# Perceiver layer on one core: first group's output projection and layer norm moved into the last sampled-attention group, set-up spreads moved to GpSimd

## What is computed

```
x = x + xattn(ctx, ctx, layernorm(x))   # K, V, Q projections; 5 sampled keys a query; softmax; @ Wo.T + bo
x = x + attn(layernorm(x))              # q, k, v = short_conv(h @ W); 2 chunks of 16 rows, carried W_in, W_out; @ Wo
x = x + ffn(layernorm(x))               # the expert of the largest gate score

def short_conv(x, w):
    xp = jnp.pad(x, ((0, 0), (KSIZE - 1, 0), (0, 0)))
    y = sum((w[:, j] * xp[:, j:j + l, :] for j in range(KSIZE)))
    return y + x
```

## Time and profile before

| what | value |
|---|---|
| median of three runs | 1219.58 us (1213.76 to 1223.68) |
| profiled execution | 1217.85 us, span 1216.1 us |
| TensorE busy, mean granted clock | 1061.4 us (87% of the span), 0.904 |
| VectorE, ScalarE, GpSimd busy | 813.3, 494.7, 320.2 us |
| SyncE's first transfer of the sampled attention, the fast weights, the experts | 115.55, 482.96, 1087.55 us from the span's start |

### The profile page before, as it was taken

The page is one execution under the profiler, slowest core; times in us unless marked ns, Lnnn a source line. Parts: engine busy times, 40 slices in busy tenths (PEclk is TensorE's granted clock), DMA queues, the critical chain, the costliest instruction groups (busy, mean ns, idle before and its releaser), DMA issues. The chain is left out here.

```text
span 1216.1 us, 18598 instructions
## 1 busy us (share of the span) xinstructions
PE 1061.4 (87%) x6220; PEld 787.6 (65%) x6220; DVE 813.3 (67%) x1592; ACT 494.7 (41%) x954; POOL 320.2 (26%) x265
## 2 busy tenths in 40 slices
PE   5993999999999963698999999999999987875997
PEld 4883566666666652477878776968696876763443
DVE  4565286778778883357888787979688876633332
ACT  1220255776676774134444443434252534310110
POOL 0344376677577662000000000000000000011553
PEclk9997898989889975788999999999899987765999
DMA  4281410222021000100010101010010031046541
GB/s 153 87 333 59 82 42 1 59 58 57 2 58 35 18 18 32 56 1 35 1 53 1 53 2 54 1 53 2 2 53 1 18 105 70 36 159 261 158 144 58
DMA packets 59924, 75.12 MB, mean 62 GB/s; under 512 B 37758, under 2 KB 42302, under 8 KB 57792
## 3 DMA queue, kind: packets, MB, share of 16 engines
q1 hardware_dynamic: 52384, 53.05, 13.7%
q0 software_dynamic: 5152, 12.59, 3.2%
q10 hardware_dynamic: 2304, 8.39, 1.7%
HBM read 56.71 MB, written 22.81 MB: 65 GB/s over the span
## 5 line engine op out<-in xcount | busy, mean ns | idle before, releaser
L1196 POOL COPY fw_x<-fw_x 128x1024 f32<-128x1024 f32 x8 | 8.3, 1040 | 536.0 <-DMA xh_scr<-fw_x 502.4
L556 POOL TENSOR_TENSOR aw_wtent<-aw_tent,aw_e 128x1760 f32<-128x1760 f32 x32 | 100.7, 3145 | 114.1 <-DVE aw_e L552 114.1
L745 PE MATMUL aw_psum_kv<-all_xWv,aw_c 128*128 128x512 f32 x256 | 124.6, 633 | 0.0
L528 POOL TENSOR_TENSOR aw_tent<-all_const,all_ix 128x1760 f32<-128x1760 f32 x32 | 100.6, 3145 | 5.1 <-POOL aw_wtent L556 4.6
L851 ACT ACTIVATE aw_cT<-aw_psum_av 32x256 f32<-32x256 f32 x128 | 80.5, 629 | 38.7 <-PE aw_psum_av L774 37.6
L733 PE MATMUL aw_psum_kv<-aw_c,all_xWk 128*128 128x352 f32 x256 | 81.6, 474 | 9.5 <-POOL aw_A L632 9.5
L2020 PE MATMUL ex_psum_y<-ex_We,ex_gT 128*128 x184 | 85.0, 607 | 0.0
L745 PEld LDWEIGHTS aw_psum_kv<-all_xWv,aw_c 128*128 128x128 f32 x256 | 49.4, 203 | 52.9 <-issue 51.1
L539 DVE TENSOR_TENSOR aw_prod<-aw_tent,aw_psum_s 128x1760 f32<-128x1760 f32 x32 | 63.5, 1984 | 23.8 <-ACT aw_tent L534 17.3
L1510 PE MATMUL fw_psum_front<-all_xWo,fw_cT 128*128 128x512 f32 x128 | 66.0, 666 | 11.7 <-DMA fw_cT<-c_scr 11.4
L733 PEld LDWEIGHTS aw_psum_kv<-aw_c,all_xWk 128*128 128x128 f32 x256 | 49.0, 196 | 35.2 <-POOL aw_A L632 9.6
(11 more groups left out here) (265 smaller groups left out, 2256.7 us busy)
## 6 DMA issues: line engine op xcount, KB each, us to landing
ex_We<-expert SPq DMA_DIRECT2D x1, 8192.0 KB, 22.4
aw_craw<-ctx SPq DMA_DIRECT2D x8, 704.0 KB, 4.8
xh_scr<-fw_x SPq DMA_DIRECT2D x10, 512.0 KB, 3.6
pj_x<-x_tok SPq DMA_DIRECT2D x8, 512.0 KB, 3.6
q_scr<-pj_QT ACTq DMA_DIRECT2D x8, 512.0 KB, 2.9
aw_Qb<-q_scr SPq DMA_DIRECT2D x32, 128.0 KB, 3.4
c_scr<-aw_cT ACTq DMA_DIRECT2D x8, 512.0 KB, 2.7
fw_cT<-c_scr SPq DMA_DIRECT2D x8, 512.0 KB, 4.8
```

Source lines behind the costliest of these rows:

```text
L528: return nc.gpsimd.tensor_tensor(self.tent[r][:], bc(rows, 1, self.nu * NK), bc(ix, 2, self.wr), ALU.subtract)
L556: return eng.tensor_tensor(self.wtent[:], self.tent[r][:], bc(self.e[:].rearrange("p u k -> p (u k)"), 2, self.wr), ALU.mult)
L745: mm = nc.tensor.matmul(ps_kv[:, j % 2, :], rows, Wv[:, c, :], start=(c == 0), stop=(c == KC - 1))
```

## The change

It adds a class `Lead` that owns two buffers for the whole kernel: `wide` (four tiles of 128x1024, which also serves as `Qblk[0]`, the even groups' queries of the sampled attention) and `even` (which also serves as `cw[0]`, the even groups' context). In the last group of the sampled attention, whose buffers are the odd ones, the `Lead` steps for group 0 of the fast weights are put between the group's own: loads behind the last scores of group 6, y0 and y1 into the two idle PSUM banks of `ps_kv`, addition, layer norm, transposes, copy into `hT`. The loads of group 1 are issued there too. The fast phase marks those fills as done and starts at the convolution fills. The clearing and the 16 copies go from VectorE to GpSimd; VectorE keeps the sum of convolution weights (`wsum`), which ScalarE now waits for in place of `setup`.

```
+class Lead:
+        self.cT = wide[:, 0:n].rearrange(cols, c=KC)
+        self.xs, self.x1, self.h = (wide[:, j * n:(j + 1) * n].rearrange(cols, c=TT) for j in (1, 2, 3))
+        self.hT = even[:, 0:n].rearrange(cols, c=KC)
+    def load(self, sp):
+        sp.dma_start(self.cT, self.a["c_scr"][0]).then_inc(self.c_in.sem, 16)
+        sp.dma_start(self.xs, self.a["x_lb"][0].rearrange("p t d -> p t d")).then_inc(self.x_in.sem, 16)
+        sp.wait_ge(self.x1_done.sem, self.x1_done.at(0, 1))
+        sp.dma_start(self.cT, self.a["c_scr"][1]).then_inc(self.c_in.sem, 16)
+        sp.dma_start(self.xs, self.a["x_lb"][1]).then_inc(self.x_in.sem, 16)
+        sp.wait_ge(self.c_in.sem, self.c_in.at(1, 16))
+        sp.wait_ge(self.x_in.sem, self.x_in.at(1, 16))
+    def sums(self, dve):
+            self.nc.vector.tensor_tensor(self.x1[:, j, :], ring.bank(f"y{j}"), self.xs[:, j, :], ALU.add)
+    def enter(self, dve):
+        ch.link(nc.vector.tensor_tensor(self.x1, self.x1, bc(self.k["weights"]["xbo"][:], 1, TT), ALU.add))
+        dve.sem_inc(self.x1_done.sem, 1)
+        normal_stats(nc, self.m, ch, self.x1, self.stats, self.mv, self.var, TT)
```

In `attend_window_phase`, in order SyncE, GpSimd, VectorE's `group`, TensorE's `group`, ScalarE's `group` (`last` is the last group):

```
             rounds(sp, NG, load, 1)
+            sp.wait_ge(s_ps.sem, s_ps.at(NG - 2, PAIRS))
+            lead.load(sp)
...
             m.start(pool)
+            lead.start(pool)
...
+                if last:
+                    lead.sums(dve)
                 weights(t, 3)
+                if last:
+                    lead.enter(dve)
+                    lead.entered(dve)
...
                 scores(t, 3)
+                if last:
+                    pe.wait_ge(v_cp.sem, v_cp.at(t.r, PAIRS))
+                    lead.y(pe, 0)
                 turn(t, 1)
                 context(t, 0)
+                if last:
+                    lead.y(pe, 1)
...
+                if last:
+                    lead.turned(pe)
                 context(t, 3)
...
                 context(t, 2)
+                if last:
+                    lead.deviation(act)
                 turned(t, 3)
+                if last:
+                    lead.copied(act)
...
                 context(t, 3)
```

In `fast_phase`, SyncE and GpSimd:

```
             sp.dma_start(Wg[:], a["gate"]).then_inc(wg_in.sem, 16)
-            load(FIRST)
-            load(FIRST.next())
...
             m.start(pool)
+            st = Chain(pool, slink, 0, m.settle)
+            for buf in (win0, wout0, wrow0, own0):
+                last = nc.gpsimd.memset(buf[:], 0.0)
+            st.link(last)
+            for hq in range(HQ):
+                for dst, src in ((win0, wi), (wout0, wt)):
+                    nc.gpsimd.tensor_copy(dst[rows, :, cols].rearrange("p g (b d) -> p g b d", b=BG), bc(src[rows], 2, BG))
+                nc.gpsimd.tensor_copy(own0[rows, :, hq * DI:(hq + 1) * DI], wi[rows])
+                last = nc.gpsimd.tensor_copy(wrow0[rows, :, cols], wr[rows])
+            last.then_inc(setup.sem, 1)
```

On VectorE the same memsets and copies go, and on VectorE, TensorE and ScalarE:

```
+            nc.vector.memset(top[:], 0.0)
+            nc.vector.tensor_scalar_add(wsum[:], conv[:, :, :, 3], 1.0).then_inc(weighed.sem, 1)
-            enter(FIRST)
-            entered(FIRST)
+            front.skip_reads(dve, "dve", 0, "y0", "y1")
...
-            ahead(FIRST, *[x for x, _ in FRONT])
+            front.skip(pe, 0, "y0", "y1", "t0", "t1")
+            ahead(FIRST, *[x for x, _ in FRONT[4:]])
             pe.wait_ge(setup.sem, setup.at(0, 1))
...
-            act.wait_ge(setup.sem, setup.at(0, 1))
+            act.wait_ge(weighed.sem, weighed.at(0, 1))
-            deviation(FIRST)
-            turned(FIRST)
+            front.skip_reads(act, "act", 0, "t0", "t1")
```

More of the change, by code:

```diff
@@ new lines, in lead_phase, with _ @@
+def lead_phase(nc, lead):
+    with ExitStack() as ctx:
+        lead.open(ctx)
+        block = ctx.enter_context(nc.Block())
+        @block.sync
+        def _(sp):
+            lead.load(sp)
+        @block.gpsimd
+        def _(pool):
+            lead.start(pool)
+        @block.vector
+        def _(dve):
+            lead.sums(dve)
+            lead.enter(dve)
+            lead.entered(dve)
+        @block.tensor
+        def _(pe):
+            lead.y(pe, 0)
+            lead.y(pe, 1)
+            lead.turned(pe)
+        @block.scalar
+        def _(act):
+            lead.deviation(act)
+            lead.copied(act)
@@ L585, in attend_window_phase @@
         craw = m.sb("craw", [P, KC, W * BG])
-        cw = [m.sb(f"c{p}", [P, KC, BG, 64]) for p in two]
-        Qblk = [m.sb(f"Qb{p}", [P, KC, BG, P]) for p in two]
+        cw = [k["even"][:].rearrange("p (c b m) -> p c b m", c=KC, b=BG), m.sb("c1", [P, KC, BG, 64])]
+        Qblk = [k["wide"][:].rearrange("p (c b n) -> p c b n", c=KC, b=BG), m.sb("Qb1", [P, KC, BG, P])]
         KT, V = [m.sb(f"K{p}", [P, KC, BG, W]) for p in two], [m.sb(f"V{p}", [P, PAIRS, D]) for p in two]
@@ L1080, in fast_phase @@
         front, back = Ring(m, "front", 4, FRONT), Ring(m, "back", 4, BACK)
-        cT, xs = m.sb("cT", [P, KC, GT]), m.sb("x", [P, TT, D])
-        x1 = [m.sb(f"x1{p}", [P, TT, D]) for p in range(2)]
-        h, x2 = m.sb("h", [P, TT, D]), m.sb("x2", [P, TT, D])
+        cT, xs, h, hT = lead.cT, lead.xs, lead.h, lead.hT
+        x1 = [lead.x1, m.sb("x11", [P, TT, D])]
+        x2 = m.sb("x2", [P, TT, D])
         stats, mv, rstd = m.sb("st", [P, TT, 6]), m.sb("mv", [P, TT, 2]), m.sb("rs", [P, TT])
-        hT = m.sb("hT", [P, KC, GT])
         f = [{n: m.sb(f"{n}T{p}", [P, KC, GT]) for n in "qkv"} for p in range(2)]
@@ L1189, in _ @@
             m.start(pool)
+            st = Chain(pool, slink, 0, m.settle)
[3 more added lines that the diff above has]
+            for hq in range(HQ):
+                rows, cols = slice(hq * HD, (hq + 1) * HD), slice(hq * HD, (hq + 1) * HD)
+                for dst, src in ((win0, wi), (wout0, wt)):
[3 more added lines that the diff above has]
+            last.then_inc(setup.sem, 1)
+            pool.wait_ge(setup.sem, setup.at(0, 1))
+            m.settle(pool)
             def keep(t):
@@ L1205, in _ @@
         def _(dve):
[L1206 to L1215, removed]
-            st.link(last)
-            st.link(nc.vector.tensor_scalar_add(wsum[:], conv[:, :, :, 3], 1.0))
-            nc.vector.memset(top[:], 0.0).then_inc(setup.sem, 1)
+            nc.vector.memset(top[:], 0.0)
+            nc.vector.tensor_scalar_add(wsum[:], conv[:, :, :, 3], 1.0).then_inc(weighed.sem, 1)
             def enter(t):
@@ L2042, in layer @@
         k["ones"] = k["const"][:, CONE:CONE + 1]
+        k["wide"] = m.sb("wide", [P, 4 * KC * GT])
+        k["even"] = m.sb("even", [P, 2 * KC * GT])
+        lead = Lead(nc, ctx, a, k)
         project_phase(nc, a, k)
```

98 lines of the change are left out of this document (82 added, 16 removed).

## The result

| | median us | against the kernel before (95% interval) | profiled execution: span | its first own scores, group 0 | its last, group 7 |
|---|---|---|---|---|---|
| before | 1219.3 | | 1216.1 | 535.9 | 981.4 |
| after | 1212.0 | 0.9956 (0.9936 to 0.9976) | 1210.5 | 518.3 | 971.8 |

The forecast was 1200 (1194 to 1209) and faster by more than 1%. The change gave 0.4% by the ratio (7 us by the medians), not 18 us. It is a small gain, clear of no change. The "own scores" of the table are the 8 short products at the head of each group's back in the fast weights (`own_scores`); they serve as milestones, one in each of the eight groups, from here on; the seven stretches between them are called steps.

What follows compares the result with a forecast made beforehand. It took the border's chain of single hand-overs as the bound, 28.31 us from the store's issue to the first fill. Gaining 19.5 and losing 1.1 gave 18.4 us off 1217.85: 1199.5, stated as 1200, range 1194 to 1209.

Steps and rivals of the forecast that it cites:

- Loads, y0, y1: hidden: Last sampled group: loads have 30 us; y0 and y1 fit TensorE's waits before turns 1 and 2; base cost 0.
- R1: Rival: low clock through the last sampled group; store 8.3 us late, gain 14.2, time 1204; chance 0.16.
- Store 4.1 us later: End of last sampled group: fourth context waits for the norm's transposes, so the store moves from 479.63 to 483.74.
- Entry 1.3 us: Fast weights' start: from SyncE's first transfer (487.07) to first fill (488.4), waiting for GpSimd's increments; bounds 0.55 and 3.8 us.
- within 2 us of SyncE's entry: Sign in the profile after: first convolution fill 15 to 21 us earlier and this close behind SyncE entering the phase.
- Fill at the low clock, 1.1 lost: First two convolution fills: TensorE comes from idleness, so 6.45 us instead of 5.35; loss range 0 to 1.5.
- Spreads and counters on GpSimd, 0: GpSimd's memsets and 16 copies done by 502, wanted at 517.5; eleven more base increments ahead of sampled attention: cost 0, bound 0.8.
- R3: Rival: spreads end last, 16 copies at 3.0 us ending near 543.5, `own_scores` 7.6 us later; time 1225; chance 0.04.
- R2: Rival: GpSimd and VectorE hinder each other in the front, 6 to 11 us lost, time 1206 to 1211; chance 0.08.
- the last memset was held: Head of sampled attention: GpSimd's last memset looked held until VectorE's copy ended (123.00), so starting later changes nothing.
- Sum 18.4: Whole kernel: 19.5 us gained at the first fill less 1.1 for the clock, from 1217.85 to 1199.5.
- R4: Rival: gain given back because something behind the front waits for what did not move; about 1217; 0.06 with other losses.

Runs made afterwards that it cites:

- the two profiles of after: The first is the changed kernel's profile in the result (1212.0 us); the second is from timing the same kernel again unchanged: 1211.3 us, 0.9962 against the kernel before.
- after + 32: Changed kernel with 8 more matrix products (32 TensorE instructions) in the branch that is not taken: 1198.9 us, 0.9869 against the kernel before.
- the exchanged kernel: Changed kernel with 32 TensorE instructions of padding, its two attention branches exchanged so the next phase's code follows directly: 1199.6 us, 0.9842 against the kernel before.
- after + 208: Changed kernel with 52 more matrix products (208 TensorE instructions) in the branch that is not taken: 1208.0 us, 0.9928 against the kernel before.

## Why the prediction was wrong

Its terms, one by one, in the two profiles of after:

- *Loads, y0, y1: hidden.* Right: nothing waits for a load, and turn 2 is 0.3 us earlier in the first profile, 0.9 later in the second, as the scores ahead of it are. y0 took 5.76 and 4.90 us (5.63 in the row of that shape), y1 3.70 in both; so R1 falls.
- *Store 4.1 us later.* From the fourth turn 12.0 us in both profiles, 8.0 before: 4.0. Against the span's start it is 2.6 in the first profile, whose fourth turn came 1.4 earlier, and 5.0 in the second (484.60). The chain was as told: table load behind the third context, transposes, fourth context. The table load took 1.28 us and the square root stood 0.02 us behind it; the 2.66 us of the Trainium skill ("ScalarE: Activation LUTs", "What ACT_TABLE_LOAD costs") did not show.
- *Entry 1.3 us.* 4.0 and 1.1. The bounds (0.55 to 3.8) nearly held both, but for the wrong reason: not GpSimd's increments but TensorE's code decides. The sign "within 2 us of SyncE's entry" failed in the first profile.
- *Fill at the low clock, 1.1 lost.* 6.38 us against 5.35: 1.0.
- *Spreads and counters on GpSimd, 0.* The copies took 0.19 to 0.29 us and ended at 494.3, TensorE wants them at 518.25. R3 falls. R2 was hardly put to the test: of VectorE's convolution only the first three steps, from 493.87 on, run beside GpSimd's copies, and they take 1.47 us together, as in before. The first product of the sampled attention came 1.3 us later (123.52 to 124.82); 0.4 of it is a later start of the block (115.98 for 115.55), the other 0.9 is about the bound of 0.8. So the reading that the last memset was held, and that counters ahead of it cost nothing, was wrong: TensorE waited for the memset again, 10.37 us. At the last scores of the first profile nothing is left of it (446.91, 446.61).
- *Sum 18.4.* 17.7 and 18.2 at the first own scores. That the first is so near is in part luck: the store was 1.5 us better than told and the entry 2.7 us worse. With the loop out of the way 16 to 17 us reach the end by the medians, 13.8 and 15.2 the last own scores in the profiles.

The step that failed is R4: "something behind the front waits for what did not move. I find none", with 0.06. The forecast took the phase behind the front for a rigid block that starts earlier. It looked for data that might not be there, and for engines; it did not ask for the code. The block was not rigid: its loop stood elsewhere in TensorE's stream of instructions, and that cost 8 us of the 17.7 (453.5 - 445.5). By the steps, 5.8 of the 8 lie in the two that hold TensorE's stalls of 2.7 and 2.4 us and the half clock behind them (67.5 and 66.6 us for 64.1 and 64.1), 1.4 in the step behind the first, and 0.8 in the first step, ahead of any jump, whose cause stays open. The profile of before had what was needed: code loads on queue 8 at each jump (720.8 and 849.1), and steps of 64.1 to 65.8 us from group 2 to 6, against 61.7 to 62.5 elsewhere. The Trainium skill says it as well ("Runtime: NRT & Kernel Launch", "Instruction fetch mechanics"): the next 16 KiB block is fetched in sequence, and a taken branch to a target that is not held forces a fetch ahead of execution. By that rule the jumps cost something in both kernels, and the runs without a loop agree (5.8 and 15.8 us off the seven steps).

Open: what of this is VectorE's. VectorE too has issue gaps of 3.1 to 3.4 us behind the jump, at one of the two loop ends in before and after + 32, at both in after and in the exchanged kernel; writing the loop out took both away together. The first in after and the only one in before:

```profile
715.48 0.29 DVE L1448 TENSOR_REDUCE fw_top<-fw_psum_back 128x32 f32<-128x128 f32 x1 [3.27 <-issue]
```

```profile
860.41 0.29 DVE L1306 TENSOR_REDUCE fw_top<-fw_psum_back 128x32 f32<-128x128 f32 x1 [3.14 <-issue]
```

Their price can't be read from the steps: the one behind the first loop end took 63.1 us with such a gap in after + 32, and 64.2 without it in before.

## What to carry to other kernels

An edit ahead of a hardware loop moves the loop's code, and a loop of this size (ten 16 KB loads on queue 8 a turn, in before and in after) was some 10 us faster or slower for that alone; before a change is judged, look for "issue" gaps at loop ends and phase entries, with instruction loads beside them. To measure an edit by itself, pad the branch that is not taken or write the loop out in both kernels. Where code size allows, the loop can stay written out: that gave 0.5% before and 1.4% after here.

## What the hardware showed that I had not expected

- Code that never runs changed the time by +11 us (48 instructions, in the kernel before) and by -11 us (32, in after).
- A jump to code that was not asked for costs TensorE 2 to 3 us: 3.1 between request and first instruction at the entry (486.43 to 489.58), 3.2 at a loop end of after + 208 (707.3 to 710.4), 2.2 and 2.7 at those of after. It is free where a wait for data covers it: in after + 32 the piece is asked for at 704.9 and TensorE waits for VectorE until 707.57.
- The same program took 3.8 us more or less from the last own scores to the experts, by the granted clock of one 21 us stretch (0.51 or 0.76) behind the same work at the same clock.
